# Attention steps in another order: three late units, the output projection first in a step, weight rounding moved

## The reference

```python
x = x + _L0_attn_ref(_layernorm(x), Wq, Wk, Wv, Wo, bo)
x = x + _L0_xattn_ref(ctx, ctx, _layernorm(x), ssm_kernel, D, 8)
x = x + _L0_ffn_ref(_layernorm(x), w_gate_up, w_proj)
# in _L0_attn_ref: 32 query heads, 8 key/value groups of 64
q, k = _rope(q), _rope(k)
scores = (einsum('bhsd,bhtd->bhst', q, k) + alibi) / math.sqrt(64)
probs = softmax(where(causal, 30.0 * tanh(scores / 30.0), -inf))
ctx = einsum('bhst,bhtd->bhsd', probs, v)
out = ctx.reshape(N, S, 2048) @ Wo + bo
# in _L0_ffn_ref, for groups of 64 weights in bfloat16:
scale = clip(mean(abs(w_g)), 1e-08)
w_hat = clip(round(w_g / scale), -1, 1) * scale
```

## Time and profile before

| | |
|---|---|
| median of 3 runs | 1425.08 us (1421.83 to 1427.48) |
| the profiled execution's own time | 1428.04 us |
| its span | 1426.3 us |
| PE busy | 1239.1 us, 87% |
| DVE, ACT, POOL busy | 890.3, 602.7, 686.0 us |
| mean granted TensorE clock | 0.951 |
| median from issue to landing: store of a unit, piece of Wo | 2.4, 4.1 us |
| first attention step to last output projection | 72.7 to 846.8 us |

### The profile page before, as it was taken

How to read it: one execution, slowest core, us unless ns; L and a number is a source line. 1 busy time by engine, 2 the same in 40 slices (tenths; PEclk the granted TensorE clock), 3 DMA queues, 4 the chain that set the end, 5 groups by cost and what they waited for, 6 DMA issues and landing times.

```text
span 1426.3 us, 20012 instructions
## 1 busy us (share of the span) xinstructions
PE 1239.1 (87%) x7264; PEld 835.4 (59%) x7264; DVE 890.3 (62%) x1166; ACT 602.7 (42%) x704; POOL 686.0 (48%) x576
## 2 busy tenths in 40 slices
PE   2584898989999989899998494999969999999996
PEld 1441564654655647456465243777748778777782
DVE  5753546676766666757667477889854455544543
ACT  1366547375384563854846244000014333323331
POOL 3535645473663644737447232999913232222330
PEclk9797899999999999999999797999979999999999
DMA  7263353153351522424405412777300000000000
GB/s 261 69 188 106 120 164 104 41 169 99 100 159 43 176 97 69 148 91 137 143 26 170 150 63 60 131 148 156 77 0 1 16 2 16 15 15 15 1 16 30
DMA packets 130200, 127.96 MB, mean 90 GB/s; under 512 B 31750, under 2 KB 89382, under 8 KB 130150
## 3 DMA queue, kind: packets, MB, share of 16 engines
q1 hardware_dynamic: 105196, 121.07, 27.5%
q10 hardware_dynamic: 24960, 6.29, 2.9%
HBM read 85.84 MB, written 35.21 MB: 85 GB/s over the span
## 4 chain that ended last, share of the span: by engine, by line
PE 54%; issue 13%; POOL 11%; DVE 10%; ACT 8%; DMA 2%; ACTq 0%; POOLq 0%; DVEq 0%; SPq 0%
PE bank L675 11%; PE bank L721 8%; PE bank L722 8%; POOL parts L1380 4%; PE bank L536 4%; PE bank L601 4%; PE bank L537 3%; PE bank L538 3%; PE bank L740 3%; PE bank L741 3%; POOL halves L1384 3%; ACT region_c L836 3%; POOL ctx_lo L1396 2%; PE bank L602 2%; ACT rsum L802 2%
## 5 line engine op out<-in xcount | busy, mean ns | idle before, releaser
L721 PE MATMUL bank<-h_hi,guT 128*128 128x256 f16 x1024 | 226.9, 274 | 1.4 <-DVE h_lo L1281 1.4
L722 PE MATMUL bank<-h_lo,guT 128*128 128x256 f16 x1024 | 226.8, 274 | 0.0
L536 PE MATMUL bank<-hT_hi,w_hi 128*128 128x256 f16 x640 | 177.6, 277 | 28.0 <-DVE w_lo L1067 14.6
L601 PE MATMUL bank<-region_c,v 128*128 128x512 f32 x256 | 136.6, 616 | 52.3 <-DVE ctx L1020 52.2
L537 PE MATMUL bank<-hT_lo,w_hi 128*128 128x256 f16 x640 | 177.3, 277 | 0.0
L538 PE MATMUL bank<-hT_hi,w_lo 128*128 128x256 f16 x640 | 177.2, 277 | 0.0
L1390 POOL TENSOR_SCALAR_AFFINE_SELECT region_c<-region_c 128x512 f32<-128x512 f32 x128 | 106.4, 854 | 120.9 <-ACT region_c L839 120.9
L675 PE MATMUL bank<-kv,toep 128*128 128x288 f32 x640 | 159.1, 413 | 4.3 <-POOL kv L1459 2.6
L1380 POOL TENSOR_TENSOR parts<-parts 128x512 f32<-128x512 f32 x80 | 116.9, 1462 | 92.0 <-DVE parts L999 76.7
L675 PEld LDWEIGHTS bank<-kv,toep 128*128 128x128 f32 x640 | 123.5, 193 | 39.7 <-POOL kv L1459 3.1
L1008 DVE STREAM_TRANSPOSE rsumT<-rsum 128x512 f32<-128x512 f32 x64 | 45.4, 709 | 139.2 <-ACT rsum L802 139.2
(11 more groups left out here) (130 smaller groups left out, 2638.8 us busy)
## 6 DMA issues: line engine op xcount, KB each, us to landing
unit_halves<-halves SPq DMA_DIRECT2D x80, 256.0 KB, 2.4
q_both<-unit_halves SPq DMA_DIRECT2D x64, 256.0 KB, 3.0
wffn<-wo SPq DMA_DIRECT2D x16, 512.0 KB, 4.1
q_high<-unit_halves SPq DMA_DIRECT2D x64, 128.0 KB, 3.1
wffn<-w_gu SPq DMA_DIRECT2D x8, 1024.0 KB, 5.4
toep<-kernel_padded SPq DMA_DIRECT2D x32, 256.0 KB, 4.2
cpair<-ctx_pairs SPq DMA_DIRECT2D x32, 176.0 KB, 4.5
xin<-x SPq DMA_DIRECT2D x8, 512.0 KB, 3.6
```

Of the source, the lines that this page charges most:

```text
L536: pe.matmul(dst, lh, rh, start=first and k == 0, stop=False)
L601: pe.matmul(dst, v1[:, 0, g, :], sc_first[:, n, o:REP:2, :], start=True, stop=False)
L721: pe.matmul(dst, guT[:, k, col:col + P], h3_hi[:, p, k, :], start=(k == 0), stop=False)
L722: mm = pe.matmul(dst, guT[:, k, col:col + P], h3_lo[:, p, k, :], start=False, stop=(k == DB - 1))
```

## The change

`LATE` becomes 3, so 7 units are early, and late units 7, 8 and 9 are projected in steps 2, 3 and 4. `WO_AFTER` becomes 5: `output(g-5)` stands first in steps 5 to 9, and outputs 5, 6 and 7 are left for the unit phase, the first of them behind unit 0. The share is rounded behind the copy of unit 5. Its thresholds are found in step 0 of the next attention and spread in two halves in steps 0 and 1. The digits are made in steps 3 to 5, the scales spread in steps 5 and 6, and the scaling is done in steps 7 to 9. `prepare` and `prepared` run a step earlier. On SP, the loads of Wo pieces stand between the three late units.

```diff
-LATE = 2
+LATE = 3
-        WO_AFTER = 4
+        WO_AFTER = 5
...
             place_early(0)
-            for c in range(2, 6):
+            for c in range(2, 4):
                 load_wo_next(c)
-            store_unit(0, EARLY)
-            place_unit(0, EARLY)
-            for c in range(6, O_PIECES + 2):
-                load_wo_next(c)
-            store_unit(0, EARLY + 1)
-            place_unit(0, EARLY + 1)
+            for n, ends in zip(range(EARLY, UNITS), (6, 8, O_PIECES + 2)):
+                store_unit(0, n)
+                place_unit(0, n)
+                for c in range(ends - 2, ends):
+                    load_wo_next(c)
...
+                elif n >= EARLY + TT:
+                    pe.wait_ge(unit_turned, UNITS * b + n - 1)
...
                     elif step < TT + LATE:
                         project(b, EARLY + step - TT)
+                    elif not first:
+                        output(b, step - WO_AFTER)
...
-                    if step >= WO_AFTER and not first:
-                        output(b, step - WO_AFTER)
...
-                    if n:
-                        for g in itertools.islice(left, 1):
-                            output(b, g)
+                    for g in itertools.islice(left, 1 if n else 0 if first else 1):
+                        output(b, g)
...
+                    if 2 < step < 2 + LATE:
+                        high_unit(b, EARLY + step - 2)
                     if step >= 3:
                         high_ctx(b, step - 3, first)
-                    if step == 4:
-                        high_unit(b, EARLY + 1)
-                    if step in (1, 2) and not first:
-                        spread(b - 1, gscale, DIGITS, step - 1)
+                    if step in (0, 1) and not first:
+                        spread(b - 1, gthr, THRESHOLDS, step)
+                    if step in (5, 6) and not first:
+                        spread(b - 1, gscale, DIGITS, step - 5)
...
                 if not last:
-                    round_share(b)
                     for n in range(EARLY):
                         high_unit(b + 1, n)
-                        if n == 1:
-                            spread(b, gthr, THRESHOLDS)
+                        if n == EARLY - 2:
+                            round_share(b)
...
                     if step == 0 and not first:
-                        find_digits(b - 1)
+                        find_thresholds(b - 1)
...
-                    if step == 2:
-                        rotate(b, EARLY + 1)
-                    if 2 <= step < 5 and not first:
-                        scale_digits(b - 1, step - 2)
+                    if 2 <= step < 1 + LATE:
+                        rotate(b, EARLY + step - 1)
+                    if 3 <= step < 6 and not first:
+                        find_digits(b - 1, step - 3)
+                    if 7 <= step < 10 and not first:
+                        scale_digits(b - 1, step - 7)
                     if first:
                         weigh_wo(step)
+                    if step == 5 and not last:
+                        prepare(b + 1)
                     if step == 6 and not last:
-                        prepare(b + 1)
-                    if step == 7 and not last:
                         prepared(b + 1)
...
-                        if n == 1:
-                            find_thresholds(b)
-                        if n == (EARLY - 1 if first else 3):
+                        if n == (EARLY - 1 if first else 2):
```

More of the change, by code:

```diff
@@ L343, in unit_bank @@
         def unit_bank(n):
-            return SC_BANKS[(n + 2) % 3] if n < EARLY else WO_BANKS[n - EARLY]
+            return SC_BANKS[(n + 2) % 3] if n < EARLY else WO_BANKS[(n - EARLY) % 2]
         def pv_bank(g, o):
@@ L881, in _ @@
             round_share(B - 1)
-            spread(B - 1, gthr, THRESHOLDS)
+            for part in range(2):
+                spread(B - 1, gthr, THRESHOLDS, part)
             for part in range(2):
@@ L1102, in find_thresholds, with find_digits @@
                 dve.tensor_scalar(cut, cut, -0x10000, None, ALU.bitwise_and).then_inc(quant_step, 1)
[L1104 removed]
+            def find_digits(f, part):
                 base = QUANT_STEPS * f
[L1106 to L1113 removed]
+                if part == 0:
+                    dve.wait_ge(spread_done, 4 * f + 2)
+                    dve.tensor_tensor(w_ternary, w_bf[:], w_by, ALU.is_gt).then_inc(quant_step, 1)
+                elif part == 1:
+                    dve.wait_ge(quant_step, base + THRESHOLDS + 1)
+                    dve.tensor_tensor(w_by, w_bf[:], w_by, ALU.add).then_inc(quant_step, 1)
+                    dve.wait_ge(quant_step, base + THRESHOLDS + 2)
+                    dve.tensor_scalar(w_by, w_by, 0.0, None, ALU.is_lt).then_inc(quant_step, 1)
+                else:
+                    dve.wait_ge(quant_step, base + THRESHOLDS + 3)
+                    dve.tensor_tensor(w_ternary, w_ternary, w_by, ALU.subtract).then_inc(quant_step, 1)
             def scale_digits(f, part):
@@ L1117, in scale_digits @@
                 if part == 0:
-                    dve.wait_ge(spread_done, 3 * f + 3)
+                    dve.wait_ge(spread_done, 4 * f + 4)
                     dve.tensor_tensor(w_ternary, w_ternary, w_by, ALU.mult).then_inc(quant_step, 1)
@@ L1190, in _ @@
                 if c >= 1:
-                    for n in range(2 * c, 2 * c + 2):
+                    for n in range(2 * c, min(2 * c + 2, EARLY)):
                         rotate(0, n, first=True)
@@ L1205, in _ @@
             find_thresholds(B - 1)
-            find_digits(B - 1)
+            for part in range(3):
+                find_digits(B - 1, part)
             for part in range(3):
@@ L1404, in attend @@
                 for step in range(STEPS):
-                    if step in (2, 4):
-                        add_parts(b, EARLY + step // 2 - 1)
                     if step >= 4:
                         low_ctx(b, step - 4)
+                    if 2 <= step < 2 + LATE:
+                        add_parts(b, EARLY + step - 2)
                     if step < NG:
                         mask(b, step)
-                    if step in (2, 4):
-                        low_unit(b, EARLY + step // 2 - 1)
+                    if 2 <= step < 2 + LATE:
+                        low_unit(b, EARLY + step - 2)
                     if step == 6 and not last:
```

9 lines of the change are left out of this document (removed).

## The result

| | before | after |
|---|---|---|
| median of the runs | 1426.28 us (4) | 1454.97 us (4; 1450.85 to 1457.2) |
| ratio, 95% interval | | 1.0201 [1.0164, 1.0238] |
| the profiled execution's own time, span | 1428.04, 1426.3 us | 1453.71, 1452.0 us |

The kernel became 2.0% slower. The forecast was 1467 in a range of 1445 to 1490; the sign and the range held, the middle was 12 us too high.

What follows compares the result with a forecast made beforehand. PE was taken to bound the loop (busy 85.04 of 92.10 us), but not a stretch of batch 7. Loop +16, batch 0 +5 and batch 7 +21 made +42 on 1425.1: 1467 us, range 1445 to 1490.

Steps and rivals of the forecast that it cites:

- Steps 2 to 9 of the loop: PE waits: scores(2) 1.1, values(1) 1.15, scores(7) 0.9, values(5) 2.6, values(6) 0.2, unit 0 2.25 us; none at output(3).
- Step 1: Loop pass from first value projection (T): tanh 0 until T+8.1, PE ready T+6.5, wait at scores(1) 1.6 us, was 1.9.
- The loop term, +16: Six loop passes: PE's waits 9.8 against 7.0 us, +2.8 a pass, less in the first; bounds +0 and +28.
- the rival of half clock: PE falls to half clock behind longer waits: 2.6 to 2.9 us in each pass, +17, 1484 us; 9 in 100.
- The sum: Whole kernel: 16 + 5 + 21 = +42 us, 1470 for the profiled execution, 1467 for the median.
- The tail is hidden: End of batch 7: the share's store and load cost nothing, 1467 - 13.5 = 1453 us; 7 in 100.
- Waits only move: Loop: PE's waits only change place, +0 there, 1451 us in all; 14 in 100.
- The loop gains: Loop: without the four passes beside the units and the deviation wait, all 7.0 us go, -42, 1409 us; 7 in 100.
- The lock of DVE and POOL: Step 0: moving digits out frees POOL; last units at least 1.5 us sooner by the rule, but scores(1) wait kept at 1.6.
- Batch 0, +5: First batch: one unit less in the prologue, Wo's later loads delaying tanh 6, part returned in step 7; bounds 0 and +9.
- My terms, -2.4, +7.4 and -2.3: Batch 0: -2.4 one unit less in prologue, +7.4 tanh 6 behind Wo's splitting, -2.3 back in step 7.
- Batch 7, +21: Last batch: DVE's load wait ends 1.0 later, its steps +6.5, share 7's load behind share 6's store +13.5; bounds 14, 24.

Runs made afterwards that it cites:

- Digits early: The changed kernel with the digit passes a step earlier, in steps 2 to 4 instead of 3 to 5; 1431.21 us, 1.001 of before.
- low first: The changed kernel with the next batch's low parts ahead of the second scaling pass in step 8; 1443.84 us, 1.012 of before.
- the run with Wo's loads and the outputs: Order only, with leftover outputs behind units 1 to 3 and, in batch 0, Wo pieces 2 to 5 loaded before unit 7's store; 1380.82 us, 0.966 of before.
- share 6 early: The changed kernel, but in batch 7 alone share 6 gets digits in step 2, spreads in 3 and 4, scaling in 4 and 5; 1444.07 us, 1.013 of before.
- Order only: The changed kernel with weight rounding, thresholds, digits, spreads and scaling back at their old places; 1388.74 us, 0.974 of before.
- Output first: The kernel before with one edit: output(g-5) first in steps 5 to 9 instead of output(g-4) last in steps 4 to 9; 1421.88 us, 0.994.
- three late units: The kernel before with three late units instead of two, and Wo pieces 2 to 5 loaded ahead of unit 7's store in batch 0; 1420.53 us, 0.994.
- Weights only: The kernel before with only the change's weight schedule (rounding, thresholds, digits, spreads, scaling); 1481.82 us, 1.039 of before.
- statistics early: The kernel before with only prepare and prepared a step earlier, in steps 5 and 6; 1403.98 us, 0.981 of before.

## Why the prediction came out as it did

**Steps 2 to 9 of the loop** were right in place. `scores(7)` 0.8 (forecast 0.9), `values(5)` 2.5 (2.6), unit 0 1.9 (2.25), `values(1)` 0.9 (1.15), `scores(2)` 0.8 (1.1), no wait at `output(3)`. Each was some tenths too long, and the 0.2 at `values(6)` didn't come. Digits early and low first show that the causes of the first three are the forecast ones; those of the two in steps 2 and 3 are argued.

**Step 1 failed.** "PE is ready at T+6.5: wait 1.6" at `scores(1)` became nothing (0.4 in the slower pass from 293.71), and 0.9 at `scores(0)` took its place, which I hadn't forecast. ACT in time, of the changed kernel, T = 388.62:

```profile
390.88 2.75 ACT L819 CAST w_bf<-wffn 128x3072 bf16<-128x3072 f32 x1
393.53 0.61 ACT L815 CAST halves<-parts 128x512 f16<-128x512 f32 x1
...
394.67 1.53 ACT L836 ACTIVATE region_c<-bank,cap_scale 128x1536 f32<-128x1536 f32 x1
```

Tanh 0 ended at T+7.6, not T+8.1, and PE was itself 0.9 later. It waited for the placing of unit 2. The placings follow the stores of units through one queue behind unit 0's, and three outputs now stand between the first units. That this is the cause, the run with Wo's loads and the outputs bears out, where an output less stands ahead of unit 2 and the wait at `scores(0)` is gone. I had checked that SP was free for unit 0's store and had not followed the placings behind it.

**The loop term, +16, is the one that was mis-sized.** Waits after were 7.7, not 9.8. The seven waits of the forecast were 3.0 too long together, 1.6 of it at `scores(1)` alone, and the 0.9 at `scores(0)` was missing. So a pass waits 0.7 longer than before instead of 2.8, and the six passes took 4.7 more instead of 16. PE's busy time in the six is the same in both kernels (517.4 and 517.2 us): three passes of either ran at a granted clock of 0.96 to 0.98, so the rival of half clock added nothing here, though the clock did matter in the parts.

**The sum.** In spans the kernel became 25.7 us slower, not 42. Of the difference 11.3 are the loop, 2.0 batch 0, 2.0 batch 7, and 1.0 the time behind the first stage, which I had left as it was. That the loop came out near nothing was forecast for no reason of its own: I added small waits at PE, and didn't see that they are what remains of a gain and a loss of some 40 us each.

**The rivals.** "The tail is hidden", 1453, lies nearest to the median, and its reason is wrong: the share's wait stands in the trace with 11.85, and share 6 early takes it away. "Waits only move", 1451, is near too, and its +0 is close to the loop's 4.7, but the experiments speak against its reason. Order only gained 41.8 in six passes and the weights on top took 46.5 back. Both numbers are near by luck. "The loop gains" had 7.0 in a pass; the order does 6.05 by itself, but with the four passes still in step 0, which this rival held to be the cause.

**The lock of DVE and POOL.** Moving the digits out of step 0 was not needed. In the order only they are still there; POOL in time, then DVE:

```profile
372.76 2.71 POOL L1380 TENSOR_TENSOR parts<-parts 128x512 f32<-128x512 f32 x1 [0.24 <-DVE parts L999]
```

```profile
372.59 1.75 DVE L1107 TENSOR_TENSOR wffn<-w_bf,wffn 128x3072 bf16<-128x3072 bf16 x1
374.38 2.71 DVE L1109 TENSOR_TENSOR wffn<-w_bf,wffn 128x3072 bf16<-128x3072 bf16 x1
```

The sum that starts second takes 2.71, the digit pass that starts second too. PE's waits in this pass are 1.3 in all, and the 0.8 of them at `scores(0)` goes when the outputs move behind units 1 to 3, with the digits still in step 0. In the changed kernel the wait at `scores(1)` is gone, but the copy of unit 6 stands there directly behind the rounding (393.53, above) and waits for no sum of POOL, so the lock isn't what took it away. The Trainium skill (SBUF — State Buffer, SBUF: two separate sides) says that whichever of such a pair starts first holds the shared ports for its whole instruction; these rows agree: POOL's sum starts 0.17 behind the first pass and takes 1.4 longer than the 1.27 of the earlier trace rows, and the pass that meets it running takes 0.95 longer than 1.76.

**Batch 0, +5:** +3.0. My terms, -2.4, +7.4 and -2.3, make 2.7 and not the 5 that I put into the sum. Attention 0 began 2.3 sooner, ACT stood 5.6 us in front of L790 on loads of Wo, as forecast, and tanh 6 came 8.0 later than before:

```profile
135.06 1.54 ACT L836 ACTIVATE region_c<-bank,cap_scale 128x1536 f32<-128x1536 f32 x1
```

The 7.7 that the Wo edit gives back is of that size. What I left out is the earlier `prepared`, which by itself takes 4.5 us off attention 0. Attention 0 became 5.3 longer, and 7.7 - 4.5 is 3.2, so some 2 us of it are open, and that the 2.7 of my terms is so near is in part luck.

**Batch 7, +21:** +19.0, in cause as forecast. The share's wait is 11.85 against 13.5; I had taken 5.5 from the store to the next load from the earlier trace rows, and it took 862.51 - 858.65 = 3.9. Pass 1.8, 3.9, 0.4 and 6.4 less 0.6 is 11.9. The rest is 7.1 against 7.5: DVE's wait for the load of the earlier batches ended 1.1 later (1.0 forecast), and its steps from there to the last `high_ctx` were 6.0 longer (6.5).

## What to carry to other kernels

A change that moves many things can be the sum of terms far larger than what remains of them (here in the loop a gain of 31 to 42 us and a loss of 36 to 47, of which 4.7 remained), so its parts are to be priced and tried apart: two lines for the row statistics gave 1.9% alone, and digit passes one step too late cost 23 us of the span, 1.6%. Parts that were tried alone must be tried together too, since their gains need not add. When work that frees a buffer is moved later, follow the buffer to its next load, since whatever consumes that load inherits the delay wherever nothing else stands in front of it. In an in-order queue a wait on a late event belongs where the other engines have work of their own to cover it, as the 17 us of batch 7 show.

## What the runs showed that I had not expected

- **Full clock is itself part of a gain.** Output first and three late units took some 1.6 us of waiting out of a usual pass and gained nothing there: PE's same matmuls took 86.5 to 86.7 us at clock 0.98, against 85.1 at 1.00. Weights only, with 10.5 of waits, was busy 88.9 at 0.95. Order only, with 1.3, kept 1.00 in all six passes. That the clock costs the pass its full price shows where one kernel has both: with the statistics early, passes with 4.1 to 4.3 us without work took 88.9 at 1.00 and 91.8 at 0.96. But it doesn't follow the sum of waits alone: before has passes of 7.0 us of waits at 1.00 and, with the same order of work, at 0.96. What decides it between like passes stays open.
